# Two attentions on one core: VectorE's maxima and the third score slot moved ahead of other work

## The reference, cut to what matters

```
x = x + attn0(norm(x), ctx)              # 16 heads of 16, softmax(q k' / 4) v, biases on q, k, v
x = x + experts0(norm(x))                # per token the one expert with the highest affinity
x = x + attn1(norm(x), ctx)              # 8 heads of 32, softmax(q k' / 16)
      # attn1: O = q + A v ; O = norm(O) g0 + b0 ; O = O + relu(O Wo' + bo) ; norm(O) g1 + b1
x = x + experts1(x)                      # two experts of eight per token, gated
```

## Time and profile before

| | |
|---|---|
| median of three executions | 1906.9 us (1899.91 to 1917.9) |
| the profiled execution's own time | 1913.12 us |
| its span, first to last instruction | 1911.4 us |
| busy: PE, DVE, ACT, POOL | 83%, 56%, 42%, 45% of the span |
| PE busy in attention 0's steady part (53.3 to 529.5 us) | 436.08 of 476.20 us, granted clock 1.00 |
| PE busy in attention 1's steady part (955.6 to 1453.2 us) | 435.96 of 497.60 us, granted clock 0.91 |

### The profile page before, as it was taken

The page is one execution under the profiler, slowest core; times in us unless marked ns, Lnnn a source line. Parts: engine busy times, 40 slices in busy tenths (PEclk is TensorE's granted clock), DMA queues, the critical chain, the costliest instruction groups (busy, mean ns, idle before and its releaser), DMA issues. The chain is left out here.

```text
span 1911.4 us, 48579 instructions
## 1 busy us (share of the span) xinstructions
PE 1592.3 (83%) x16482; PEld 1180.4 (62%) x16483; DVE 1067.3 (56%) x2274; ACT 812.3 (42%) x1574; POOL 851.5 (45%) x1177
## 2 busy tenths in 40 slices
PE   5999999999962999995989898888888249898868
PEld 4777777777741666664777677777777124343356
DVE  3666666666634222222576666767676556655545
ACT  3667666676640222222555454545554001111111
POOL 3666666666630111113455555545554116666500
PEclk8999999999975999997998888989898559999979
DMA  4112121100005111112112111211100202222255
GB/s 120 52 54 74 52 74 52 30 29 21 23 12 208 33 33 33 33 30 80 31 60 72 54 50 54 73 31 33 29 27 10 98 29 89 90 93 89 84 181 175
DMA packets 51897, 119.22 MB, mean 62 GB/s; under 512 B 10221, under 2 KB 28629, under 8 KB 48501
## 3 DMA queue, kind: packets, MB, share of 16 engines
q1 hardware_dynamic: 40948, 88.42, 14.2%
q0 software_dynamic: 10880, 29.90, 4.8%
HBM read 89.32 MB, written 28.97 MB: 62 GB/s over the span
## 5 line engine op out<-in xcount | busy, mean ns | idle before, releaser
L959 DVE TENSOR_REDUCE a_mx<-a_SM 100x2 bf16<-100x722 f32 x384 | 351.3, 915 | 193.1 <-PE a_SM L425 187.6
L704 ACT ACTIVATE a_Pr<-a_ST 120x1600 f32<-120x1600 f32 (+3 forms) x192 | 225.0, 1172 | 77.4 <-PE a_ST L457 75.9
L425 PE MATMUL a_SM<-a_KT,a_QM 32*100 32x362 f32 x768 | 159.0, 410 | 112.8 <-DVE a_mx L959 108.5
L753 POOL TENSOR_TENSOR a_rstd<-a_ve,a_powers 100x1 f32<-100x1 f32 x192 | 123.2, 642 | 278.3 <-DVE a_ve L929 274.9
L1717 PE MATMUL g_PH<-w,g_xT 128*128 x456 | 211.3, 607 | 20.4 <-issue 16.5
L467 PE MATMUL a_M<-a_Pr,a_V 120*32 120x100 f32 (+3 forms) x4608 | 187.9, 263 | 0.6 <-ACT a_Pr L704 0.6
L425 PEld LDWEIGHTS a_SM<-a_KT,a_QM 32*100 32x100 f32 x768 | 63.8, 162 | 180.5 <-DVE a_mx L959 149.2
L467 PEld LDWEIGHTS a_M<-a_Pr,a_V 120*32 120x32 f32 (+3 forms) x4608 | 145.7, 125 | 27.0 <-issue 23.2
L1717 PEld LDWEIGHTS g_PH<-w,g_xT 128*128 128x128 f32 x456 | 82.7, 191 | 115.0 <-issue 115.0
L1764 ACT ACTIVATE g_sg<-g_ab 128x512 f32<-128x512 f32 x57 | 35.9, 630 | 217.6 <-DVE g_ab L1792 205.9
L355 PE MATMUL a_M<-a_ch,a_wkh 128*128 128x362 f32 x256 | 101.6, 397 | 29.0 <-POOL a_cl L821 29.0
(11 more groups left out here) (204 smaller groups left out, 3707.5 us busy)
## 6 DMA issues: line engine op xcount, KB each, us to landing
w<-in_E_w SPq DMA_DIRECT2D x24, 1024.0 KB, 6.7
a_ct<-in_ctx SPq DMA_DIRECT2D x64, 362.0 KB, 3.0
g_GR<-gated_rows SPq DMA_DIRECT2D x32, 400.0 KB
keep_rows<-a_keep SPq DMA_DIRECT2D x64, 100.0 KB
tile_rows<-e_y SPq DMA_DIRECT2D x32, 128.0 KB, 1.7
b_rows<-in_E_b SPq DMA_DIRECT2D x1, 4096.0 KB
out<-g_y SPq DMA_DIRECT2D x32, 100.0 KB
X<-in_x SPq DMA_DIRECT2D x1, 2800.0 KB
```

Of the source, the lines that this page charges most:

```text
L425: last = nc.tensor.matmul(SM[0:LQ, half, 0:LKP], QM[b.p][rows, chunk, m, :], KT[b.p][rows, chunk, :], start=True, stop=True)
L704: nc.scalar.activation(Pr[0:n, s, :].rearrange("p (r q) -> p r q", r=GROUPS), ST[0:n, :, 0:PER * LQ], ACT.Exp, scale=SCALE).then_inc(exp_d ...
L753: nc.gpsimd.tensor_tensor(rstd[k][:], ve[k][:].to_broadcast([LQ, n]), powers[:, 0:n], ALU.pow).then_inc(rstd_ready[k], 1)
L959: V_.tensor_reduce(pair, SM[0:LQ, :, 0:LK], AX_X, ALU.max).then_inc(max_done, 1)
```

## The change

It moves instructions within each engine's order, and adds or removes none of the arithmetic.

- PE, layer 0: `scores(b, 2)`, then score pair 4, and only then `out_transposes`; before, the transposes stood between the two. Layer 1: `out_transposes` moves from ahead of `scores(b, 2)` to behind score pair 2, and pair 3 moves ahead of `start_k`.
- ACT, both layers: `copy_out` (the copy of the output's transposes, L675) moves from behind the second exponential to behind the third.
- DVE, layer 0: maximum 0 ahead of `residual_stats`; the input's statistics are cut in two, with maximum 2 between them. Layer 1: `tail1a` behind maximum 0, `tail1c` behind maximum 1, and `end1(prev2, 0)` and `input_stats(nxt2)` behind maximum 2.

```diff
 class Links:
-    def __call__(self, instruction):
+    def counted(self, instruction):
         instruction.then_inc(self.sem, 1)
         self.n += 1
+
+    def settled(self):
         self.engine.wait_ge(self.sem, self.base + self.n)
+
+    def __call__(self, instruction):
+        self.counted(instruction)
+        self.settled()
...
 # PE, step
                 rows_of(*((3,), ())[layer])
-                if tail and layer == 1:
+                if back:
+                    scores(b, 2)
+                rows_of(*((4,), (2,))[layer])
+                if tail:
                     if fr:
                         pe.wait_ge(v_evac, nxt.count(2, 1))
-                    out_transposes(prev, True, prev.low >= LAG)
-                if back:
-                    scores(b, 2)
-                if tail and layer == 0:
-                    if fr:
-                        pe.wait_ge(v_evac, nxt.count(2, 1))
-                    out_transposes(prev, False, True)
-                rows_of(*((4,), (2,))[layer])
+                    out_transposes(prev, layer == 1, prev.low >= LAG)
                 if back:
                     values(b, 1)
...
-                rows_of(*((6,), ())[layer])
+                rows_of(*((6,), (3,))[layer])
                 if ahead:
                     start_k(nxt, nxt2, prev, tail)
-                rows_of(NP - 1)
+                rows_of(*((7,), ())[layer])
...
 # ACT, step
+                    if tail and s == 2:
+                        prev = b.plus(-1)
+                        copy_out(prev, 0, RC + DC if prev.low >= LAG else DC)
                     if tail and layer == 0 and s == 2:
                         kept(b.plus(-1))
-                    if tail and s == 1:
-                        prev = b.plus(-1)
-                        copy_out(prev, 0, RC + DC if prev.low >= LAG else DC)
...
 # DVE
             def norm_stats(k, b, src):

+                moments(src)
+                variance(k, b)
+
+            def moments(src):
+                wait_apart()
+                link.counted(V_.bn_stats(st[:], src))
+
+            def variance(k, b):
+                link.settled()
                 if k in APPLIED:
                     dve.wait_ge(nmr_ready[k], b.count(1))
-                wait_apart()
-                link(V_.bn_stats(st[:], src))
                 wait_apart()
                 link(V_.bn_aggr(mv[k][:], st[:]))
...
 # DVE, step0
-                if tail:
-                    residual(prev)
-                    residual_stats(prev)
                 for j in range(NP):
                     if tail and j == 6:
                         take_product(prev, False, True)
                     if fr:
                         maxima(nxt, j)
+                    if tail and j == 0:
+                        residual(prev)
+                        residual_stats(prev)
                     if ahead and j == 1:
-                        input_stats(nxt2)
+                        moments(xrow(nxt2))
+                    if ahead and j == 2:
+                        variance(0, nxt2)
...
 # DVE, step1
                 if tail:
                     residual(prev)
                     residual_stats(prev)
-                    tail1a(prev)
                 for j in range(NP):
                     if fr:
                         maxima(nxt, j)
                     if tail and j == 0:
+                        tail1a(prev)
+                    if tail and j == 1:
                         tail1c(prev)
-                    if ends and j == 1:
+                    if ends and j == 2:
                         end1(prev2, 0)
-                    if ahead and j == 0:
+                    if ahead and j == 2:
                         input_stats(nxt2)
```

## The result

The changed kernel takes 1895.7 us (median of 8 executions, 1884.43 to 1899.27). The kernel before took 1910.64 in executions beside it (8, 1899.91 to 1917.9). The ratio is 0.9913, with a 95% interval of 0.9886 to 0.994: 15 us less, where 38 were forecast. The profiled execution took 1896.2 us, its span is 1894.4.

A forecast was written before the change was run, and what follows sets the result against it. Attention 1 was taken as bound by a four-engine ring, 17.54 us a step with `tail1a` held. Gains of 24 us there and 14 in attention 0 took 1906.9 to 1869 us; 8-in-10 range 1842 to 1906.

The forecast's parts named there:

- Attention 0: First attention stretch: earlier maxima shorten PE's waits before pairs 1 and 3; 14 us gained, bounds 5 and 18.
- the slot's move: In attention 0, transposes and their copy move behind the third exponential; effect put at nothing.
- Attention 1: Second attention stretch: step falls from 18.43 to 17.54 us over 27 steps, 24 us gained.
- the wait of 2.00 us: PE's wait before score pair 1 in attention 1's long steps, claimed removed because maximum 0 now precedes `tail1a`.
- The ring: Attention 1 dependency cycle through PE, DVE, GpSimd and ACT, claimed to bound the step: 17.03 us, 17.54 with `tail1a` held.
- The block of `tail1a`: In attention 1, GpSimd's L821 holds this DVE instruction to about 1.3 to 1.7 us, adding 0.51 us a step.
- Short steps: The faster of attention 1's alternating loop steps, 16.5 us before, forecast to get slower by 1.0 us.
- rival 4: Attention 1's waits move to ACT, steps stay near 18.4 us; attention 0 loses its gain: 1895 to 1907; chance 0.10.
- Rivals 2: Attention 1's clock stays half in part, costing about 0.8 us a step, 22 us: 1891; chance 0.14.
- rival 3: Idle of 2.2 to 2.8 us halves the clock in every attention 1 step: slower, 1928 or more; chance 0.12.
- a clock below 0.95: Sign of being wrong in attention 1, pointing to the two lower-clock rivals; the forecast expected near 1.00.
- steps that still alternate: Sign of being wrong: attention 1 steps not all near 17.5 us, meaning the loop branch is not absorbed.

The follow-up runs named there:

- resid_early: Changed kernel with attention 1's residual addition on VectorE moved from the head of a step to the end of the step before, ahead of the loop branch: 1845.9 us, ratio 0.9672.

## Why the prediction was wrong

**Attention 0: right.** 15 us in the 29 steps it counted instead of 14, all from VectorE's order, and the slot's move at nothing, as put. PE's waits for maxima between 100 and 500 us fell from 27.3 us, the longest 0.5, to 16.2, the longest 0.3.

**Attention 1, the failed step.** It is the sentence "What is removed: the wait of 2.00 us, since PE reaches avs' transposes with maximum 3 already taken and maximum 0 stands ahead of `tail1a`". The wait of 2.00 did not come from `tail1a`. It came from the addition (L993) that the branch delays into L812, and the change leaves that instruction, its branch and its place alone. The prediction had said so itself from the earlier trace rows, "in the long step its loop branch delays L993, which then takes 1.74 us", and "everything behind it, maximum 0 too, is late", and then priced only the instruction that had moved, `tail1a` against L821. With the change the wait is 1.51 us instead of 2.00, shorter by about the size of `tail1a`, and the half clock, which the prediction expected to go "with them", stays and grows: 0.88 over the 27 steps instead of 0.91. Attention 1 takes 18.57 us a step where 17.54 was forecast. Without the meeting the kernel takes 1845.9 or 1845.6.

**The ring: right in its mechanism, and its term was mis-sized by 0.56 us.** With the meeting gone, a step is 16.98 us where 17.54 was forecast. Cut in the forecast's pieces, in `resid_early`: L406 at 1074.25 to pair 2 at 1082.71, 8.46 instead of 8.29 + 0.51 = 8.80; pair 2 at 1065.73 to the last statistics at 1071.04, 5.31 instead of 0.45 + 0.83 + 0.55 + 3.77 + 0.07 = 5.67; from there to L406 at 1074.25, 3.21 instead of 2.05 + 1.02 = 3.07. The block of `tail1a` came (1.37 us, within the 1.3 to 1.7 forecast) but cost pair 2 only 0.25. That error would have been worth 15 us on the good side; it is not why the forecast failed.

**Short steps.** They were to rise to 17.5 with the long ones. They fell to 15.5; as I read it, the long step before gives the ring time, and everything but PE is early after it. Only the mean of both kinds could be compared with the ring, 18.57 over the 27 steps, and that is above it.

**The rivals.** "The waits only move" (rival 4) came nearest in time, 1895 to 1907, by a mechanism it did not name. Rivals 2 and 3 had the lower clock as their price, which was right (0.88 instead of 0.91), and thin idle time, for rival 3 the ring's, as its cause, which `resid_early` shows to be wrong for 25 steps. Rival 3's figures for that price, 2.2 to 3.8 us a step at most, were too small as well: 23.40 against a step of 16.85 is 6.5. Of the signs of being wrong that the prediction gave, two appeared: a clock below 0.95, and "steps that still alternate (the loop branch is not absorbed)". The second points at the cause.

**The rule of the port.** The Trainium skill, page "SBUF — State Buffer", section "Who interferes with whom", has "Issue order, not op shape, decides who blocks." The runs agree in that a held VectorE instruction ends 0.28 or 0.29 us behind GpSimd's end (1.30 to 2.53 us instead of 0.42 to 0.48), that GpSimd takes 1.88 instead of 1.74 when it comes second, and that the maximum with its one input is never held: the 384 of each trace took 0.90 to 0.92 us. They add that the start in the record is not the order meant: 0.44 us ahead by the record was held, 0.17 ahead passed. The same skill's page "Advanced Engine Details and Errata", section "Sequencer Loop", says that engine instructions are read and queued and then wait for their semaphores. A turn that is taken in the queue, before the record begins, would fit it; no run here shows the queue.

## What to carry to other kernels

When a wait is late because of one instruction, follow it to the first late instruction and ask whether the change touches that one; here the moved maximum stood ahead of the wrong neighbour. The steps with two long gaps gave back their lost clock here only when both were gone, so price them together, and a gain in idle time (22 us here) that leaves one gap of 1.5 us can come back as nothing. Look for the swap that takes a late input out of a ring: one exchange of two instructions on an engine 44% busy was worth 89 us of the 103 gained.

## What the hardware showed that was not expected

- A wait of 1.2 to 1.8 us of PE was followed, in the loop's steps shown here, by the level of 1.2 GHz for 3.4 to 13.5 us, and steps of 18.1 to 23.4 us instead of 15.4 to 17. With pieces of up to 1.0 the clock stayed whole through 25 steps. The length of one piece does not tell by itself: 1.18 in the short steps of before left the clock whole, so did 1.98 and 1.42 in one long step, and the last step of `resid_early` lost it without a wait over 0.8 us.
- A short idle time of VectorE, its loop branch of 0.72 us once in two steps, made the difference: written out (`dve_flat`), the changed kernel is 50 us shorter. With the ring cut it matters little: 1806.7 us with the branch where it was, 1801.4 without it and with the early addition.
- A two-input VectorE instruction of 0.42 us can take 2.45 although its record starts 0.44 us ahead of GpSimd's, and 0.43 when it starts 0.17 ahead. The one thing found to differ is whether GpSimd's input was ready by then; in 175 steps this sorts all but a few at the edge.
